# Pairwise attention layer of a graph network: the mask of a tile made by GpSimd, on a signal given as VectorE begins the minimum of the tile before

## The reference

```
mask = jnp.where(adj > 0, 0.0, -1e22)
q = feat @ W1.T;  k = feat @ W2.T                      # 64 features each
e = relu(q[:, None, :, :] + k[:, :, None, :])
scores = jnp.einsum('bijd,d->bij', e, a)
att = softmax(scores + mask, axis=-1);  out = att @ feat
```

## Time and profile before

| | |
|---|---|
| Median of three runs | 12305.15 us |
| The profiled execution | 12303.05 us, of which the span from its first to its last instruction is 12301.3 us |
| TensorE clock granted | 0.995 of full speed |
| PE busy | 11965.8 us, 97% |
| DVE busy | 10281.1 us, 84% |
| ACT busy | 9346.4 us, 76% |
| POOL busy | 458.4 us, 4% |
| Chain that ended last | DVE 52%, PE 45%, issue 1% |

### The profile page before, as it was taken

The page is one execution under the profiler, slowest core; times in us unless marked ns, Lnnn a source line. Parts: engine busy times, 40 slices in busy tenths (PEclk is TensorE's granted clock), DMA queues, the critical chain, the costliest instruction groups (busy, mean ns, idle before and its releaser), DMA issues.

```text
span 12301.3 us, 239883 instructions
## 1 busy us (share of the span) xinstructions
PE 11965.8 (97%) x106113; PEld 5936.3 (48%) x106113; DVE 10281.1 (84%) x12373; ACT 9346.4 (76%) x7633; POOL 458.4 (4%) x636
## 2 busy tenths in 40 slices
PE   7999999999999999999999999999999999999999
PEld 3333853338433384333843348433484334843348
DVE  4999849998599975999759997599975999759997
ACT  3898739987499874988748887489874898749986
POOL 1000000000000000000000000000000000000000
PEclk9999999999999999999999999999999999999999
DMA  2000320003200031000310003100031000310003
GB/s 74 19 21 22 105 80 22 18 22 113 76 18 18 24 117 69 18 18 26 125 59 18 18 27 132 52 18 18 31 137 43 18 22 29 140 38 19 21 32 106
DMA packets 206087, 609.72 MB, mean 50 GB/s; under 512 B 45440, under 2 KB 137216, under 8 KB 139520
## 3 DMA queue, kind: packets, MB, share of 16 engines
q1 hardware_dynamic: 184176, 450.72, 10.5%
q0 software_dynamic: 20880, 143.66, 3.1%
HBM read 556.47 MB, written 8.39 MB: 46 GB/s over the span
## 4 chain that ended last, share of the span: by engine, by line
DVE 52%; PE 45%; issue 1%; ACT 0%; SPq 0%; DMA 0%; POOL 0%; DVEq 0%
DVE E L881 34%; PE ps L1339 10%; DVE E L889 9%; PE ps L1443 8%; PE ps L1359 7%; PE ps L1456 4%; PE ps L1516 4%; PE ps L1423 4%; PE ps L1372 4%; DVE T L904 2%; PE ps L1502 2%; DVE E L879 1%; DVE HW L915 1%; DVE adj_ring L896 1%; PE ps L1322 1%
## 5 line engine op out<-in xcount | busy, mean ns | idle before, releaser
L611 ACT ACTIVATE E<-QB,KBP 128x2048 f32<-128x2048 f32 x3328 | 6398.1, 1994 | 740.0 <-PE ps L1359 722.3
L1359 PE MATMUL ps<-E,s_win 128*32 128x512 f32 x61440 | 6739.6, 594 | 104.0 <-DVE E L889 60.5
L881 DVE TENSOR_SCALAR E<-QA,KLO,KHI 128x2048 f32<-128x2048 f32 x4096 | 5252.8, 1339 | 20.0 <-DVE nmin L904 17.8
L1359 PEld LDWEIGHTS ps<-E,s_win 128*32 128x32 f32 x61440 | 1975.5, 110 | 4667.3 <-issue 4182.8
L1013 DVE CUSTOM_DVE_ANT_0 T<-ps,adj_ring 128x2048 f32<-128x2048 f32 x512 | 1171.6, 2288 | 88.9 <-PE ps L1423 86.2
L889 DVE SCALAR_TENSOR_TENSOR E<-QB,KBN,E 128x2048 f32<-128x2048 f32 x512 | 1200.3, 2344 | 0.0
L643 ACT ACTIVATE T<-T,nmin 128x2048 f32<-128x2048 f32 x512 | 1028.8, 2009 | 215.5 <-DVE nmin L1013 215.4
L1443 PE MATMUL ps<-ident,T 128*128 128x128 f32 x8192 | 1098.7, 277 | 15.7 <-DVE HT L975 12.3
L1443 PEld LDWEIGHTS ps<-ident,T 128*128 128x128 f32 x8192 | 913.5, 141 | 198.9 <-ACT PT L523 71.1
L523 ACT ACTIVATE AGG<-ps 128x512 f32<-128x512 f32 x224 | 126.7, 596 | 1012.5 <-PE ps L1339 980.9
L1339 PE MATMUL ps<-adj_res,H 128*128 128x512 f32 x2048 | 889.5, 592 | 0.0
(11 more groups left out here) (147 smaller groups left out, 7706.3 us busy)
## 6 DMA issues: line engine op xcount, KB each, us to landing
adj_ring<-in_adj SPq DMA_DIRECT2D x384, 1024.0 KB, 5.0
adj_res<-in_adj POOLq DMA_DIRECT2D x128, 1024.0 KB, 6.4
qcur<-AGG SPq DMA_DIRECT2D x896, 16.0 KB, 2.7
qcur<-HT SPq DMA_DIRECT2D x896, 16.0 KB, 2.2
HW<-in_x POOLq DMA_DIRECT2D x9, 1024.0 KB, 6.5
X<-in_x SPq DMA_DIRECT2D x128, 64.0 KB, 1.9
out_x<-X SPq DMA_DIRECT2D x8, 1024.0 KB, 16.9
wq_r<-in_L_gnn_Wq SPq DMA_DIRECT2D x4, 64.0 KB, 2.3
```

What stands on the lines that cost most here:

```text
L611: last = nc.scalar.activation(E[:, e_slot(t, k) + g, :], QB[:, :], ACT.Relu, bias=KBP[:, col:col + 1])
L881: last = nc.vector.tensor_scalar(dst, QA[:, :], KLO[:, col:col + 1], KHI[:, col:col + 1], ALU.max, ALU.min)
L1359: last = mm(ps[QROWS * g:QROWS * (g + 1), 4 * u + c, :], win, E[:, s + g, c * CH:(c + 1) * CH], start=(k == 0), stop=(k == NS - 1), tile_p ...
```

## The change

VectorE no longer makes the mask. GpSimd makes it, with the same operation over the same buffer. The counter that nobody read becomes a signal, `min1_on`: DVE raises it once the waits ahead of the minimum are met, just before the minimum. GpSimd makes the mask of tile t when the minimum of tile t-1 has been signalled (for tile 0 as soon as its rows are loaded) and goes on to the next; the inverse roots of the first three row groups are put after the masks of tiles 4, 8 and 12.

```diff
+            def mask1_tile(b, t, u):
+
+                if t:
+                    pool.wait_ge(min1_on, b * NT + t)
+                ring_wait(pool, b, 0, t // 2, u)
+                nc.gpsimd.tensor_scalar(ring[:, u, :], ring[:, u, :], 0.0, MASK_ADD, ALU.is_le, ALU.mult
+                                        ).then_inc(mask1, 1)
+
             def batch(b, more):
...
-                for k in range(LN_EARLY, LN_MID):
+                for t in range(NT):
+                    mask1_tile(b, t, t % 2)
+                    if t in (4, 8, 12):
+                        rstd_step(b, LN_EARLY + t // 4 - 1)
+                for k in range(LN_EARLY + 3, LN_MID):
                     rstd_step(b, k)
...
-            def mask1_tile(b, T, half, u):
-
-                ring_wait(dve, b, 0, half, u)
-                nc.vector.tensor_scalar(ring[:, u, :], ring[:, u, :], 0.0, MASK_ADD, ALU.is_le, ALU.mult
-                                        ).then_inc(mask1, 1)
-
             def min1(T, u):
 
                 dve.wait_ge(e_used, (T + 1) * NS)
                 dve.wait_ge(mask1, T + 1)
-                alone(dve)
+                dve.sem_inc(min1_on, 1)
                 nc.vector.tensor_tensor_reduce(
...
                         finish1(t - 1, T - 1, 1 - u)
-                    if k == 13:
-                        mask1_tile(b, T, t // 2, u)
```

More of the change, by code:

```diff
@@ L314, in build @@
         t1_rdy = sem("t1_rdy")
+        min1_on = sem("min1_on")
         p1_rdy = sem("p1_rdy")
```

## The result

The changed kernel takes 12822.2 us (median of four runs, 12819.9 to 12823.0) against 12305.2 before: ratio 1.042, 95% interval 1.0402 to 1.0438. It is 517 us slower, where 30 us less were forecast, and outside the range.

A forecast was written before the change was run, and what follows sets the result against it. PE and DVE were taken as nearly full, with PE holding plain minima after 0.24 us. Gain 30 us, no stall: 12303.05 - 30 = 12273, plus 2.1 for the median, 12275 us; range 12255 to 12440.

The forecast's parts named there:

- What is L?: Step estimating POOL's time for the 2048-column mask from nearest profile rows: 2.3 us taken, between 1.86 and 4.4 us.
- L: The time of one mask instruction on POOL, taken as 2.3 us.
- d: Time DVE is held behind the minimum by each mask: L - 2.44 us if above zero; forecast 0, 120 times.
- Who waits: At DVE's next TENSOR_SCALAR behind the minimum: POOL, once under way, keeps the shared port pair and DVE waits.
- Rival 3: At the TENSOR_SCALAR behind the minimum, POOL yields and DVE slips in: 12275 us whatever L is; chance 0.08.
- The window: From the start of DVE's minimum to its next TENSOR_SCALAR: 2.44 us in which POOL's mask costs nothing.
- Rival 1: Mask outlasts its window, holding DVE's first TENSOR_SCALAR behind the minimum: L 3.6 us, 139 us lost, 12414 us; chance 0.31.
- Rival 2: Mask slightly outlasts its window behind the minimum: L 2.5 to 2.9 us, 12282 to 12330 us; chance 0.14.
- The gain: Taking the mask off DVE ahead of the woven minima saves 3.8 us a batch, 30 us in all.
- The slack of a plain tile: Ahead of a plain tile's minimum, DVE can gain only 0.24 us before PE is what it waits for.
- The mask of tile 0: POOL's first mask of a batch falls in front of the attention layer, where DVE reads PSUM or waits: no cost.
- Rival 4: Signal comes too early, POOL enters between step 1's TENSOR_SCALARs ahead of the minimum: 132 us lost, 12407 us; chance 0.04.

## Why the prediction was wrong

- *The step that failed is "What is L?"* It took 2.3 us from AFFINE_SELECT, "nearest in kind", with 4.4 us as the upper end; L is 7.17 us, so d is not 0 but 4.31 us, 120 times. A row of 128 columns with a guessed fixed part carried a figure for 2048 columns of another instruction. Neither the MEMSET (0.86 ns a column, and 2.0 us over 2048 as measured, close to the 1.86 read) nor the add bounded it, because the cost hangs on the pair of steps: from 2.0 to 7.2 us in one and the same TENSOR_SCALAR. A bound needs an argument why nothing lies beyond it, and "reads two inputs, the mask one" was none. The range did not even reach that bound: 4.4 us would give 12305 + 235 - 30 = 12510 us. No run timed AFFINE_SELECT over 2048 columns, so whether its row was scaled wrongly or was the wrong kind stays open.
- *Who waits* was right for this operation: behind it DVE stands until near its end, at the signal (4.31 us) and without it (6.76 us). The rule of the Trainium skill (SBUF — State Buffer, "SBUF: two separate sides"), that the first to start keeps the shared port pair for its whole instruction, agrees with the trace in these tiles. It does not in 77 of the 120 tiles with a mask of 1024 columns, where a TENSOR_SCALAR of DVE took its usual 1.35 us in the middle of POOL's instruction. Rival 3, that DVE slips in and the mask costs nothing, is out for this kernel, though DVE can get in ahead of POOL's end, as the shorter mask shows; the row that I had read for it, a TENSOR_SCALAR beside an inverse root, had an operation of four numbers.
- *The window* of 2.44 us was right; 0.15 us of earlier start and 0.27 us of earlier release add to it.
- *Rival 1* was the case that came, with a chance of 0.31: the mask outlasts its window and holds the first TENSOR_SCALAR behind the minimum. Its reason for a long L was wrong, though: two passes at the MEMSET's rate would make two multiplications as long as the mask, and they take 2.0 us. So its price was wrong too, 109 us net where it is 517. With L = 7.17 its d would have been 4.73 and the net loss 568 - 30 = 538 us. Rival 2 goes with its L of 2.5 to 2.9.
- *The gain*: 30 us forecast, 26 measured with no mask. The slack of a plain tile is 0.14, not 0.24 us; PE binds through the buffers of step 1. The 1.13 us of tile 0 came as forecast, and so did the nothing of tiles 5, 9 and 13 (60.01 us apart in both).
- *The mask of tile 0* in front of the layer was called free, which it is up to some 4 us of L; at 7.09 it costs 2.90 us a batch, 23 us.
- *Rival 4*, an early signal that makes DVE wait ahead of the minimum, did not come: POOL starts 0.15 us ahead of the minimum, and the two TENSOR_SCALARs before it take 2.60 us as ever. The signal is early once a batch, at the minimum of tile 0, where DVE comes later than PE: POOL starts 0.41 us ahead there (1.27 with 512 columns). Even then it is POOL that waits, its instruction takes 7.44 us (3.14) in place of 7.17 (2.01), and the stall stays at 4.3 us.
- The estimate of some 2 us from the Trainium skill (GPSIMD Engine Reference, Engine selection, one-input work "roughly line-rate") holds here for a copy and for pairs of additions and multiplications, 2.0 us. It does not hold for this pair, which takes 3.6 times as long, nor for a single step, 5.5 us.

## What to carry to other kernels

A window for another engine's work is worth what its operation takes there: time that very instruction, with both its steps and its full width, before building a signal around it, since the whole excess can become a stall of the other engine (here 4.3 us, 120 times). Before paying for a saving, work out what the next wait leaves of it: 145 us of mask on the chain were worth 26. Where a third engine has idle time at its waits, as ScalarE had here, try the work there first.

## What the runs showed of the hardware

- On GpSimd, 128x2048 f32: a MEMSET, a copy, and a TENSOR_SCALAR of two additions or multiplications 2.0 us; a TENSOR_TENSOR 3.7; a TENSOR_SCALAR of one step 5.5, more than of two multiplications; with a comparison, maximum or minimum in a pair 7.2.
- The stall of VectorE is written into the duration of the stalled instruction (5.67 us at most for one of 1.34), not into its idle time; the list of waits does not name GpSimd.
- While GpSimd's TENSOR_SCALAR over 2048 columns is in work, no TENSOR_SCALAR of VectorE gets ahead of it (120 of 120 signals; the first one takes 5.66 to 5.67 us in 119 of them, 5.32 in one). Over 1024 columns one does in 77 of 120, and GpSimd's instruction then takes 4.83 us in place of 3.72.
- The minimum that reads PSUM and one buffer of SBUF takes 2.28 us beside a 7.17 us operation of GpSimd, as without it: nothing is lost there.
